# A graph layer with a routed expert layer on one core: router and experts in two parts of 35 and 14 node blocks, the first part's experts run between the blocks of the second during their gather

## The reference

```python
def gnn(x, W, edge_row, edge_col, edge_val):
    h = jnp.einsum('nd,od->no', x, W)
    msgs = edge_val[:, None] * h[edge_col]
    return jax.ops.segment_sum(msgs, edge_row, num_segments=N_NODES)

def ffn(x, gate_w, gate_b, w1, b1, w2, b2, gamma, beta):
    topk_vals, topk_idx = jax.lax.top_k(x @ gate_w + gate_b, 2)
    topk_w = softmax(topk_vals)
    h = relu(einsum('bsh,ehf->bsef', x, w1) + b1)          # H = 256, F = 512
    expert_out = einsum('bsef,efh->bseh', h, w2) + b2
    y = x + sum(topk_w[..., None] * take_along_axis(expert_out, topk_idx))
    return layernorm(y) * gamma + beta

x = x + gnn(layernorm(x), W, src, dst, edge_weight)       # edge_row = src, edge_col = dst
x = x + ffn(layernorm(x)[None], ...)[0]
```

## Time and profile before

| | us |
|---|---|
| median of 3 runs | 2297.76 (2297.62 to 2298.76) |
| profiled execution | 2296.52 |
| its span, first to last instruction | 2294.6 |
| PE busy | 1563.0 (68%) |
| DVE busy | 1112.2 (48%) |
| ACT busy | 362.4 (16%) |
| POOL busy | 1138.8 (50%) |
| mean granted clock | 0.782 |

### The profile page before, as it was taken

One profiled execution on the slowest core, in us unless ns is written; L12 is line 12 of the kernel. 1 busy time (PEld: TensorE's weight loads), 2 busy tenths in 40 slices (PEclk: granted clock), 3 DMA queues, 4 the chain that ended last, 5 costly groups with the idle time before them and its releaser, 6 DMA issues. The chain is left out here.

```text
span 2294.6 us, 39255 instructions
## 1 busy us (share of the span) xinstructions
PE 1563.0 (68%) x7134; PEld 1105.0 (48%) x7135; DVE 1112.2 (48%) x2894; ACT 362.4 (16%) x918; POOL 1138.8 (50%) x1147
## 2 busy tenths in 40 slices
PE   1406888857877778787777777766519999989400
PEld 1206787733433343343333334336518989978300
DVE  8899999923333333333333333325413433333387
ACT  0101000000000000000000000005414445434222
POOL 0001222337777777777777777764752222222154
PEclk7757888857788777878878887875559999999755
DMA  5101000013333333333333333341443232253442
GB/s 171 48 16 35 3 4 4 4 57 106 104 105 105 104 105 103 106 104 105 105 104 106 104 105 105 104 92 57 157 146 104 70 101 75 88 188 102 129 144 96
DMA packets 133376, 210.59 MB, mean 92 GB/s; under 512 B 36820, under 2 KB 95387, under 8 KB 133208
## 3 DMA queue, kind: packets, MB, share of 16 engines
q0 software_dynamic: 51808, 137.97, 20.2%
q1 hardware_dynamic: 69176, 56.38, 8.3%
q10 hardware_dynamic: 12352, 15.76, 2.2%
HBM read 164.79 MB, written 44.80 MB: 91 GB/s over the span
## 5 line engine op out<-in xcount | busy, mean ns | idle before, releaser
L695 POOL DMA_INDIRECT hbuf<-xn_rows,ix x832 | 793.3, 953 | 274.2 <-issue 236.5
L745 PE MATMUL bank<-hbuf,pick 128*128 x1742 | 702.9, 511 | 238.8 <-SPq L674 116.2
L745 PEld LDWEIGHTS bank<-hbuf,pick 128*128 128x128 f32 x1742 | 319.7, 227 | 604.4 <-issue 600.3
L709 DVE TENSOR_SCALAR pick<-iota_f,row_f,wgt_f 128x128 f32<-128x128 f32 x444 | 162.9, 370 | 357.8 <-PE bank L745 326.1
L612 PE MATMUL bank<-work 128*128 128x128 f32 x1568 | 232.3, 319 | 144.6 <-DVE work L517 144.6
L709 DVE TENSOR_SCALAR pick<-iota_next,row_f,wgt_f 128x128 f32<-128x128 f32 x427 | 156.1, 371 | 347.4 <-PE bank L745 298.7
L612 PEld LDWEIGHTS bank<-work 128*128 128x128 f32 x1568 | 224.8, 232 | 152.1 <-issue 149.1
L338 POOL DMA_INDIRECT edge_groups<-work,dest_i x56 | 78.5, 1402 | 387.3 <-ACT work L364 360.4
L1260 PE MATMUL bank<-xtT,w_sb 128*128 128x128 f32 x1744 | 215.5, 277 | 15.8 <-issue 14.3
L1260 PEld LDWEIGHTS bank<-xtT,w_sb 128*128 128x128 f32 x1744 | 212.2, 193 | 26.9 <-issue 22.1
L1270 PE MATMUL bank<-w_sb,hT 128*128 128x256 f32 x872 | 206.7, 380 | 0.0
(11 more groups left out here) (205 smaller groups left out, 1340.3 us busy)
## 6 DMA issues: line engine op xcount, KB each, us to landing
xt<-slots SPq DMA_DIRECT2D x110, 132.0 KB
w_sb<-in_L_ffn_w_dram ACTq DMA_DIRECT2D x28, 512.0 KB, 4.6
hbuf<-xn_rows,ix POOLq DMA_INDIRECT x832, 2.8
ya<-expert_out SPq DMA_DIRECT2D x7, 896.0 KB, 5.3
yb<-expert_out SPq DMA_DIRECT2D x7, 896.0 KB, 7.4
x<-in_x_dram SPq DMA_DIRECT2D x6, 896.0 KB, 11.1
xn_rows<-xn SPq DMA_DIRECT2D x4, 896.0 KB, 4.0
out_dram<-o SPq DMA_DIRECT2D x7, 512.0 KB, 2.9
```

The lines of the kernel that those rows point to most:

```text
L695: pool.indirect_dma_start(hbuf[:, k, :], None, xn_dram, bass.IndirectOffsetOnAxis(ap=ix[:, k:k + 1], axis=0)).then_inc(gathered[k], 16)
L709: return v.tensor_scalar(picks[n][:], rows[:], row_f[:, ds(s, 1)], wgt_f[:, ds(s, 1)], ALU.is_equal, ALU.mult)
L745: return nc.tensor.matmul(bk[q][:, 0:D], picks[k][:], hbuf[:, ds(s & (GR - 1), 1), :].rearrange("p k d -> p (k d)"), start=False, stop=Fal ...
```

## The change

Stretches 2 to 4 become one Block, and their loops over windows and experts are written out, so that every engine has the same order of work, given by `in_order`. Windows 0 to 34 with router batches 0 to 4 are part 0, windows 35 to 48 with batches 5 and 6 part 1. Each part has its own region of `slots`, its own counts and tiles, and its own expert_out, and goes through all 16 experts. A batch's router steps follow its last window by two to four windows; the last batch of a part is done in `flush`. Windows 0 to 34 and flush(0) come first, then windows 35 and 36, then part 0's experts with windows 37 to 48 between them, one after most experts, flush(1) after expert 13, and at last part 1's experts.

Rows in `slots` have 256 columns. y is stored by plain transfers in the order of `slots`, tile after tile, and yrow_i (function locate) holds for each node the two rows where its results lie; the closing pass gathers them with indirect transfers. POOL no longer has work in the experts. ACT issues the filler stores of all experts, the loads of xt and the stores of y; rows_i holds the row in `slots` of each tile. The up matmuls have two banks (UP) for four, hT waits are finer, y_sb and xtT have one buffer each, and the two normalized copies of the router are xn2 itself, which the experts' loop no longer makes. The first weights, b2, gamma and beta are loaded at the gather's start.

```diff
+    SEGS = [(0, 5), (5, WT)]
+    SIZES = [(b1 - b0) * WB * P for b0, b1 in SEGS]
+    CAPS = [n + P for n in SIZES]
+    MAXTS = [2 * n // P + EX for n in SIZES]
+        SPLIT = SEGS[1][0] * WB
+        AHEAD = 2
+        LATE = 2
+        REST = 2
+        def in_order(window, flush, begin, expert, finish):
+            for w in range(SPLIT):
+                window(w)
+            flush(0)
+            w = SPLIT
+            while w < SPLIT + AHEAD:
+                window(w)
+                w += 1
+            begin(0)
+            for e in range(EX):
+                expert(0, e)
+                while w < min(NW, SPLIT + AHEAD + (e + 1) * (NW - SPLIT - AHEAD) // (EX - LATE)):
+                    window(w)
+                    w += 1
+                    if w == NW:
+                        flush(1)
+            finish(0)
+            begin(1)
+            for e in range(EX):
+                expert(1, e)
+            finish(1)
+        AGG, TURNS, SUMS, XT, DOWN, UP = bk[0:2], bk[2], bk[3], bk[4], bk[5], bk[6:8]
...
             @block.gpsimd
+                for t in range(last):
+                    upto = rings_to(pool, SPLIT + 1 if t == last - 1 else (t + 1) * WB + 5)
+                    with pool.Fori(at, upto) as i:
+                        body(i)
+                    at = upto
+                    scatter(t)
+                scatter(last)
                 rings = pool.value_load(rings_i[0:1, 0:1], min_val=2, max_val=TT // GR)
-                body(0)
-                with pool.Fori(1, rings) as i:
+                with pool.Fori(at, rings) as i:
                     body(i)
+                for t in range(*SEGS[1]):
+                    scatter(t)
...
             @block.vector
+                def flush(g):
+                    t = SEGS[g][1] - 1
+                    add((t + 1) * WB - 2)
+                    add((t + 1) * WB - 1)
+                    factors(t)
+                    choose(t)
+                    place(t)
...
+                def expert(g, e):
...
+                    with dve.Fori(lo, hi) as s:
+                        dve.wait_ge(up_done, (s + base) * FB + FB)
+                        turned(s + base + 1)
+                        dve.wait_ge(down_done, s + base + 2)
+                        dve.wait_ge(y_sent, (s + base) * 16 + 16)
+                        dve.sem_inc(dve_steps, 1)
+                        v.tensor_tensor(y_sb[:], DOWN[:, 0:D], b2_b[:, e, :], ALU.add).then_inc(y_ready, 1)
...
             @block.tensor
+                def window(w):
...
+                    if w - 1 >= begins(w):
+                        turn(w - 1)
+                    if w - 2 >= begins(w):
+                        project(w - 2)
+                    with pe.Fori(tail, end) as s:
+                        tile(s, q, 2)
...
+                    if w - 3 >= begins(w) and batch_ending(w - 3) is not None:
+                        gate(batch_ending(w - 3))
+                    if w - 4 >= begins(w) and batch_ending(w - 4) is not None:
+                        rank(batch_ending(w - 4))
...
+                def expert(g, e):
+                    q = e % 2
+                    lo, hi = expert_tiles(pe, g, e)
+                    n = 16 * ((g * EX + e) // 2 + 1)
+                    pe.wait_ge(w1_in[q], n)
+                    pe.wait_ge(w2_in[q], n)
+                    with pe.Fori(lo, hi) as s:
+                        pe.wait_ge(xtT_ready, s + base + 1)
+                        for f in range(FB):
+                            pe.wait_ge(hT_ready, (s + base) * FB + (f + 1))
+                            for b in range(NB):
+                                m = nc.tensor.matmul(UP[f % 2][:, 0:P], w1_sb[:, q, b, f * P:(f + 1) * P], xtT[:, b, :],
+                                                     start=b == 0, stop=b == NB - 1)
+                            m.then_inc(up_done, 1)
+                        turn_tile(s + base + 1)
+                        pe.wait_ge(y_ready, s + base + 1)
+                        for f in range(FB):
+                            pe.wait_ge(hT_ready, (s + base) * FB + (f + 3))
+                            m = nc.tensor.matmul(DOWN[:, 0:D], hT[:, f, :], w2_sb[:, q, f, :], start=f == 0, stop=f == FB - 1)
+                        m.then_inc(down_done, 1)
...
             @block.scalar
+                def flush(g):
...
+                    for e in range(EX):
+                        count = act.value_load(counts_i[0:1, g, e:e + 1], min_val=0, max_val=SIZES[g])
+                        act.dma_start(slots_dram[ds(count + (ROW0[g] + e * CAPS[g]), P), :], filler[:]).then_inc(filled[g], 16)
...
+                def begin(g):
...
+                    act.wait_ge(sent[g], 16 * K2 * (SEGS[g][1] - SEGS[g][0]))
+                    act.wait_ge(filled[g], 16 * EX)
...
+                    with act.Fori(part_tiles(act, g), MAXTS[g] + 1) as s:
+                        act.dma_start(y_dram[g][ds(s * P, P), :], filler[:]).then_inc(spared[g], 16)
...
+                def expert(g, e):
+                    q = e % 2
+                    lo, hi = expert_tiles(act, g, e)
+                    with act.Fori(lo, hi) as s:
+                        for f in range(FB):
+                            act.wait_ge(up_done, (s + base) * FB + (f + 1))
+                            act.wait_ge(down_done, s + base + 1)
+                            act.activation(hT[:, f, :], UP[f % 2][:, 0:P], ACT.Relu,
+                                           bias=b1_cols[:, e * FB + f:e * FB + f + 1]).then_inc(hT_ready, 1)
+                        ahead = row_of(g, s + REST)
+                        act.wait_ge(xt_turned, s + base + REST)
+                        act.dma_start(xt[:], slots_dram[ds(ahead, P), :]).then_inc(xt_in, 16)
+                        act.wait_ge(y_ready, s + base + 2)
+                        act.dma_start(y_dram[g][ds(s * P, P), :], y_sb[:]).then_inc(y_sent, 16)
+                    if g == 0 or e + 2 < EX:
+                        act.wait_ge(down_done, hi + base + 1)
...
+                        load_w1(act, (e + 2) % EX, q)
+                        load_w2(act, (e + 2) % EX, q)
...
             @block.gpsimd
+                def fetch(t):
+                    q = t % 2
+                    if t >= 2:
+                        pool.wait_ge(y_summed, t - 1)
+                    pool.sem_inc(pool_steps, 1)
+                    for k, to in enumerate((ya[q], yb[q])):
+                        for j in range(WB):
+                            pool.indirect_dma_start(to[:, j, :], None, y_dram[seg_of(t * WB)],
+                                                    bass.IndirectOffsetOnAxis(ap=yrow_i[:, t * WB + j, k:k + 1], axis=0)).then_inc(y_in[q], 16)
...
+                fetch(0)
+                fetch(1)
+                for t in range(WT):
+                    if t + 2 < WT:
+                        fetch(t + 2)
+                    scale(t)
```

More of the change, by code:

```diff
@@ L648, in gnn_moe_kernel @@
+        y_ready = sem("y_ready")
+        located = sem("located")
+        spared = [sem(f"spared{g}") for g in range(2)]
+        y_sent = sem("y_sent")
         BIAS = 2
         HALF = GR // 2
-        def window_pairs(engine, window):
-            for w in range(4):
-                window(w, w % 2)
-            with engine.Fori(2, NW // 2) as i:
-                window(i * 2, 0)
-                window(i * 2 + 1, 1)
-            window(NW - 1, 0)
+        SPLIT = SEGS[1][0] * WB
+        AHEAD = 2
@@ L735, in _ @@
-                with dve.Fori(1, NW // 2) as i:
-                    window(i * 2 + 1, 1)
-                    window(i * 2 + 2, 0)
-                for w in range(NW - 3, NW):
-                    add.q = w % 2
-                    add(w)
+                    if w - 2 >= begins(w):
+                        add(w - 2)
+                        if batch_ending(w - 2) is not None:
+                            factors(batch_ending(w - 2))
+                    if w - 3 >= begins(w) and batch_ending(w - 3) is not None:
+                        choose(batch_ending(w - 3))
@@ new lines, in finish @@
+                def finish(g):
+                    if g == 0:
+                        tiles = part_tiles(dve, 0)
+                        dve.wait_ge(xtT_ready, tiles + 1)
+                        dve.sem_inc(xtT_ready, REST - 1)
+                        dve.wait_ge(y_ready, tiles + 1)
+                        dve.sem_inc(y_ready, REST)
+                v.memset(filler[:], 0.0).then_inc(filler_set, 1)
+                v.memset(carry_f[:], 0.0)
+                v.memset(carry[:], 0.0)
+                for g in range(2):
+                    v.tensor_scalar(expert_base[:, g, :], iota_f[:, 0:EX], float(CAPS[g]), float(ROW0[g]), ALU.mult, ALU.add)
@@ new lines, in flush @@
+                def flush(g):
+                    nonlocal sums_free
+                    t = SEGS[g][1] - 1
+                    w = (t + 1) * WB - 1
+                    turn(w)
+                    project(w - 1)
+                    project(w)
```

(27 more changed lines are left out.)

921 lines of the change are left out of this document (414 added, 507 removed).

## The result

The changed kernel takes 2663.7 us (median of 4 runs, 2655.7 to 2669.1) against 2298.3 beside it: a ratio of 1.159 [1.156, 1.162], 365 us more. It was run a second time later: 2661.8 us, 1.160 [1.157, 1.162]. The forecast was 2577. Its narrow range, 2500 to 2640 with a chance of 0.60, missed by 24 us; the wide one, 2440 to 2690, holds the time, 87 us above the forecast.

A forecast was written before the change was run, and what follows sets the result against it. It took POOL to bound the gather, PE the experts, a chain the router and DVE the closing pass. 493 + 804 + 107 + 639 + 59 + 36 + 8 + 220 + 3 + 205 = 2574, forecast 2577, range 2500 to 2640.

The forecast's parts named there:

- (c): Expert tile: ACT's store of y ahead of the next relu makes it 4.9 us instead of 3.73.
- Rival 1: Expert tiles: ACT's issue is hidden and tiles stay at 3.73 us, total 2430; chance 0.17.
- (b): First seam, to the first expert tile: router batch 4 alone on PE, POOL's ring full, then scatters; 107 us.
- (e): Second seam, the second flush: 36 us as at the first, but with 16 filler stores on ACT, 59.
- (g): Closing pass: 98 indirect gathers make POOL the bound; 205 us, bounds 186 and 235.
- (f): Second part's experts: 40 tiles x 4.9 = 196, changes 12, late weights 12; 220 us, plus 3 for the stage's end.
- (d): Overlapped stretch: 74 tiles at 4.9, 14 changes, 12 windows, batch 5's gate 25, clock 20; 639 us.
- the row above (f): Between second flush and second part: seven tiles and two changes 36 us, ACT's look-ups and first load 8.
- Rival 2: Clock stays low through the mix, 0.79 as in the gather instead of 0.99; total 2697; chance 0.17.
- (a): First part, 35 windows: POOL stays the bound with gathers and scatters; 804 us, ending at 1297.
- Rival 3: Windows 37 to 48: waits of adds and expert tiles fill each other; 397 us for 639, total 2280; chance 0.03.

The follow-up runs named there:

- number 1: Changed kernel, but in the second part SP instead of ACT loads xt and stores y: 2602.4 us, ratio 1.131.
- Number 5: Changed kernel with three buffers for the experts' weights instead of two, ACT still issuing: 2661.4 us, ratio 1.156.
- number 2: Changed kernel with four banks for the second part's up matmuls, ACT still issuing: 2604.9 us, ratio 1.135.
- number 9: Changed kernel with a ring of 32 gathered tiles for 16, expert 0's second bias for all: 3152.3 us on the slower chip; again 2619.8 beside the changed kernel's 2661.8.
- numbers 7 and 8: Changed kernel with windows 37 to 48 and flush(1) before the first expert: 2713.8 us; changed kernel split into 42 and 7 blocks: 2696.5 us.
- Number 6: Changed kernel, second part with SP issuing rows, stores and weights, four up-matmul banks, three weight buffers: 3055.3 us on the slower chip, ratio 1.154.
- number 10: Changed kernel with plain SP loads of consecutive (wrong) rows in the closing pass instead of 98 POOL gathers: 2593.0 us, ratio 1.127.

## Why the prediction was right, and where the 87 us are

**Right, by its own steps.** (c): the mechanism is the one written down, store and register work ahead of the relu, third up block waiting for it. The relu comes 1.38 us behind the start of y, forecast 1.41; the third block is 1.81 behind it in both. Only what follows was left out: behind that block the tile takes 3.35 us instead of 3.10 in the earlier trace rows; why was not taken apart. So 4.9 was 5.15, 30 us over 121 tiles. Rival 1 (the issue is hidden, 2430) is refuted by the 5.15 and by number 1. The Trainium skill (DMA: Bandwidth & Descriptors, section Issuing engines are not separate DMA queues), which calls the issuing engine's time usually small, is right about the instruction, 0.36 us, and would have missed the cost, 1.06 us per tile, because a relu that PE waits for stands behind it.

**Right in part by luck.** (b), (e) and (g) came within 10 us, and POOL was the bound of the closing pass. But (g)'s 205 holds 16 for POOL and DVE slowing each other and 6 for a tail. POOL works without a wait until 2639.8, 178 us from its first closing gather and close to the 183; what follows is 23 us, and DVE's two-input instructions were not slowed by the gathers (see the last section). Two errors of opposite sign make the 200.

**The failed terms: changes of expert, and no clock in (f).** The prediction read some 1.4 us per change in the kernel before, and then put 0.8 over a tile for the changed kernel without giving a reason, and 1.5 more for eight that wait for weights: 24 in all for (f). The second part's 15 changes average 8.94 us from y to y (134.1 together), 3.8 over a steady tile. They have two parts.

At full clock a change takes 7.34 us (from 2282.36 and from 2340.73), 2.2 over a steady tile. The last one, behind which no weights are left to load, takes 6.22 (from 2451.20). So about 1.1 is ACT's two weight issues, and 1.1 the look-ups of the next expert's bounds and the rest of what stands ahead of the first relu. That makes 32 for the 15, 8 more than forecast. The step that failed is the sentence that put the weight loads' cost at their landing; the rule of the same prediction, that every instruction on ACT ahead of a relu counts, was applied to the store and not to them. In the timeline above they hold the relu back until 2360.95, 3.56 us behind the start of y. Number 5 shows that landing is no part of it.

The other twelve changes take 8.80 to 10.15 us, because PE's pulses in them are longer: 25 us together beyond 7.34 each. This is the larger part, and the prediction had no term for it in (f): it had set its 20 us for the clock into (d). With the tiles' 0.25 (39 steps, 10 us) these are 43 of (f)'s 45.

The 10 us in the row above (f) are in part of the same kind: from the first part's last y (2180.43) to the second part's first up matmul (2193.09) pass 12.7 us where 8 were put, with two weight issues and five spare stores on ACT ahead of the first row load.

**The clock.** Rival 2 (0.79 through the mix, 2697) is refuted where it was placed: the mix has 0.93 and steady tiles are at full clock. But half of it is true elsewhere: in runs of single tiles the clock falls behind PE's waits, 0.67 in 2357 to 2398, and the step is 10.1 us where 7.34 is seen at full clock. In number 2, where PE's longest wait for ACT is 2.4 us, such a run is granted 1.00 from 2310 to 2348 and its changes take 6.2 to 6.7; the row of that stretch:

```profile
2310.00:2348.00 38.00, 25.96 (x164) 21.57 (x164) 6.83 (x18) 6.84 (x24) 0.00 (x0) 1.00 0.65 208
```

The Trainium skill (TensorE: Matmul & The Clock Gate, section HAM oscillation) ties falls to long idle gaps, and this pair agrees with it; the prediction had set it aside because of the gather's short gaps. The length of one gap does not decide it alone, though. In the changed kernel, PE's timeline at two other changes:

```profile
2286.34 1.16 PE L1209 MATMUL bank<-xtT,w_sb 128*128 128x128 f32 x8 [3.35 <-ACT hT L1312]
2406.96 1.30 PE L1209 MATMUL bank<-xtT,w_sb 128*128 128x128 f32 x8 [2.62 <-ACT hT L1312]
2408.48 3.26 PE L1216 MATMUL bank<-w_sb,hT 128*128 128x256 f32 x8
```

Behind the wait of 3.35 us the eight matmuls take 1.16, full clock; behind the one of 2.62 the clock falls, and the down matmuls take 3.26 us for 1.89. The changed kernel's second run and the second of number 9, whose second part is unchanged, have the same changes hit, so it is not chance from run to run; what decides it stays open.

**The windows, (a), (b).** (d) holds 60 steady steps, 309 us, 2 plain changes, 16, and 11 steps with one of the windows 37 to 47, 302, with 7 to the first y and 19 for window 48. Less the tiles in them, windows, changes and batch 5's gate come to 270, forecast 256; the tiles' 0.25 add 18 (74 x), the first y 2, and the 20 set aside for the clock were hardly used: +15. (a)'s stalls were put at 4; number 9 takes 12 us off them. (b)'s were named (POOL's ring full, the scatters after the missing gathers) and were 10 longer. By number 9 this one arrangement, a ring too short for the gates and the flush, costs some 42 us altogether, with what is said there of the edit's other effects.

**Rival 3** (not slower) had the overlap save PE's waits. It does save, by numbers 7 and 8 some 5 us a window, which is about what a change of expert costs since the split. Against the kernel before, the 365 us are about 172 for the tiles' 1.42 us (121 x), 45 for 12 more tiles, 55 for the closing pass, and the rest, about 90, changes of expert and the two seams less what windows no longer cost POOL.

## What to carry to other kernels

An overlap puts work into the engines' fixed orders, so for each instruction that PE waits for, count all that its engine now issues ahead of it, at the ends of the loops as well as inside them (here 1.06 us per tile and, at full clock, 2.2 over a tile per change of expert). A buffer between the bound engine and one that pauses must hold the pause: the ring held 17.6 us, the flush kept PE from its next window for 41 (1318.5 to 1359.7), and the kernel with twice the ring took 42 us less. Two remedies for one wait don't add, and behind the wait removed stands the next one (here the landing of the weights). A wait of PE can cost twice, once as itself and once by the clock behind it: here 25 us that no list of waits shows.

## What the runs showed of the hardware

**One chip runs the loops of windows slower, and nothing else that was compared.** On it the kernel before took 2650 us. Number 6's first four steps with a window in the mix take 35 to 36 us, the changed kernel's 25 to 27. Its expert tiles are 5.15 and 3.73 us as elsewhere, its first gather starts at 494.42 (495.59 in the changed kernel), and from its last y to the end it takes 205.8 us (205.7). The register operations at the line of the adds, on PE's weight sequencer, from 600 to 1250 us, first in the changed kernel and then in number 9 on the slower chip (durations in ns, min/median/max):

```profile
L1079 PEldq FUSED_REGOPS  x479: 46/46/51, 600.7 to 1249.9; - x160
```

```profile
L1079 PEldq FUSED_REGOPS  x357: 3/46/1422, 601.2 to 1247.7; - x179
```

and PE's waits there, again in this order:

```profile
PE bank L1079 <- issue: 24.1, 94, 1.1
```

```profile
PE bank L1079 <- issue: 189.3, 101, 7.4
```

The register operation's median is the same 46 ns, but some take up to 1.4 us, and PE is kept up to 7.4 us by nothing that the profile shows. What it is was not settled; it hits the loops over edge tiles and not those over expert tiles, whose bounds are in registers too.

**DVE's two-input instructions are slowed by POOL's multiplications and additions, not by its gathers.** The prediction added 16 us in (g) for the slowing. One of the two groups of such instructions, first in the changed kernel and then in number 10, with plain loads (busy us, mean ns | idle before):

```profile
L1452 DVE SCALAR_TENSOR_TENSOR o<-yb,second_w,ya 128x256 f32<-128x256 f32 x49 | 20.0, 480 | 0.2
L1458 DVE SCALAR_TENSOR_TENSOR o<-yb,second_w,ya 128x256 f32<-128x256 f32 x49 | 40.2, 886 | 0.2
```

The pass has 98 of them in all. Sorted by what POOL did for more than half of their time, in the changed kernel 60 beside a gather average 480 ns, 11 beside an idle POOL 477, and only 3 lie beside its multiplications and additions, at 2163. In number 10 there are 25 of these, at 2214, and 67 beside an idle POOL at 476; in the kernel before 38 at 1543. The one-input statistics take about 412 ns in all three. So the seven of 7.42 us in the earlier trace rows were slow for POOL's arithmetic, and with the gathers in between, DVE's 212 instructions take 72.4 us (the last row of the table at the top) where number 10 has 110.7:

```profile
2458.00:2590.00 132.00, 0.00 (x0) 0.00 (x0) 110.69 (x212) 26.93 (x56) 54.74 (x26) 0.50 0.44 144
```
